# Cross-attention with a routed expert layer on one core: each head's division and transposition moved a slot further back, and six other steps moved with them

## What is computed

```python
def attention(q, k, v):                       # once for the image keys, once for the text keys
    scores = jnp.einsum('bqhd,bkhd->bhqk', q, k) / sqrt(HD)
    return jnp.einsum('bhqk,bkhd->bqhd', softmax(scores), v)
q = rms_norm(linear(layernorm(x), q_w, q_b), norm_q_w)
k, k_img = rms_norm(linear(ctx_txt, ...)), rms_norm(linear(ctx_img, ...))
x = x + linear(attention(q, k, v) + attention(q, k_img, v_img), o_w, o_b)
w = softmax(layernorm(x) @ Wg + bg);  topv, topi = top_k(w, 2)
x = x + sum over the two experts of topv * (W3(gelu(W2(gelu(W1 layernorm(x))))))
```

## Time and profile before

| | us |
|---|---|
| median of 3 runs (837.31 to 839.81) | 837.37 |
| the profiled execution, its own time | 834.9 |
| its span | 832.7 |
| TensorE busy in the span (93%) | 770.6 |
| VectorE busy (72%) | 599.6 |
| ScalarE busy (59%) | 490.9 |
| GpSimd busy (29%) | 240.4 |

### The profile page before, as it was taken

How to read it: one execution, slowest core, us unless ns; L and a number is a source line. 1 busy time by engine, 2 the same in 40 slices (tenths; PEclk the granted TensorE clock), 3 DMA queues, 4 the chain that set the end, 5 groups by cost and what they waited for, 6 DMA issues and landing times.

```text
span 832.7 us, 17460 instructions
## 1 busy us (share of the span) xinstructions
PE 770.6 (93%) x5995; PEld 666.4 (80%) x5995; DVE 599.6 (72%) x1269; ACT 490.9 (59%) x1136; POOL 240.4 (29%) x302
## 2 busy tenths in 40 slices
PE   4889898999999989787899999999999999999994
PEld 3667676767676767555798999999999999999993
DVE  6767878787978787776676757676676758676664
ACT  4377777767676777786245555554545555554543
POOL 3523334342434333223300505032140505032010
PEclk9989999999999999999999999999999999999998
DMA  9820102011020201142756665748566665648561
GB/s 308 291 83 4 56 6 58 38 35 61 24 72 13 83 13 35 31 175 89 260 203 223 233 232 208 248 172 285 191 248 220 238 233 210 250 172 286 194 220 64
DMA packets 29205, 126.28 MB, mean 152 GB/s; under 512 B 4204, under 2 KB 4220, under 8 KB 19424
## 3 DMA queue, kind: packets, MB, share of 16 engines
q1 hardware_dynamic: 23696, 109.80, 37.6%
q0 software_dynamic: 5456, 15.81, 5.3%
HBM read 108.42 MB, written 18.74 MB: 153 GB/s over the span
## 4 chain that ended last, share of the span: by engine, by line
PE 71%; DVE 11%; ACT 10%; issue 4%; DMA 1%; POOL 0%; SPq 0%; ACTq 0%; DVEq 0%; POOLq 0%
PE tiles L1176 6%; PE tiles L1178 6%; PE tiles L1177 6%; PE scores L1478 4%; PE scores L1480 4%; PE scores L1479 4%; PE ptb L1291 4%; PE pvb L1178 3%; PE pvb L1177 3%; PE ptb L1177 3%; PE pvb L1176 3%; PE ptb L1176 3%; PE ptb L1178 3%; PE scores L1281 2%; ACT scr L658 2%
## 5 line engine op out<-in xcount | busy, mean ns | idle before, releaser
L920 DVE TENSOR_TENSOR w<-scr,w 128x2048 fp32r<-128x2048 f32 x75 | 170.8, 2288 | 59.5 <-ACT w L684 59.5
L684 ACT ACTIVATE w<-scr 128x2048 fp32r<-128x2048 f32 x76 | 144.8, 1909 | 54.8 <-PE scores L1480 54.8
L514 POOL DMA_INDIRECT out_dram<-scr,tok x17 | 18.0, 1058 | 298.7 <-DVE scr L1155 296.2
L666 ACT ACTIVATE scr<-scr,rsum 112x257 f32<-112x257 f32 x128 | 66.7, 521 | 60.6 <-DVE rsum L904 60.6
L1176 PE MATMUL tiles<-w 128*128 128x256 f32 (+1 forms) x288 | 82.9, 288 | 0.6
L1176 PE MATMUL tiles<-c,w 128*128 128x258 f32 (+2 forms) x272 | 79.3, 291 | 2.6 <-DVE c L1129 1.2
L1177 PE MATMUL tiles<-w 128*128 128x256 f32 (+1 forms) x288 | 81.2, 282 | 0.0
L1178 PE MATMUL tiles<-w 128*128 128x256 f32 (+1 forms) x288 | 81.2, 282 | 0.0
L1143 DVE CAST w<-scr 128x256 fp32r<-128x256 f32 (+1 forms) x144 | 41.9, 291 | 52.5 <-ACT scr L774 52.5
L1178 PE MATMUL tiles<-c,w 128*128 128x258 f32 (+2 forms) x272 | 76.9, 283 | 0.0
L1177 PE MATMUL tiles<-c,w 128*128 128x258 f32 (+2 forms) x272 | 76.7, 282 | 0.0
(11 more groups left out here) (223 smaller groups left out, 2332.0 us busy)
## 6 DMA issues: line engine op xcount, KB each, us to landing
scr<-in_dram SPq DMA_DIRECT2D x76, 1024.0 KB, 4.9
scr<-in_dram SPq DMA_DIRECT2D x8, 750.0 KB, 4.6
scr<-slots_d SPq DMA_DIRECT2D x10, 528.0 KB, 5.4
scr<-in_dram SPq DMA_DIRECT2D x10, 512.0 KB, 8.8
slots_d<-rows SPq DMA_DIRECT2D x8, 528.0 KB, 11.1
xn<-in_dram SPq DMA_DIRECT2D x9, 256.0 KB
xb<-in_dram SPq DMA_DIRECT2D x8, 224.0 KB, 2.7
xr<-in_dram SPq DMA_DIRECT2D x8, 224.0 KB, 2.6
```

The source lines that it names most:

```text
L666: act.activation(probs[0:L, s, 0:IMG], probs[0:L, s, 0:IMG], ACT.Copy, scale=rsum[0:L, g, s, 0:1]).then_inc(S["normal_img"], 1)
L684: act.activation(EH[slot], raw[slot], ACT.Copy).then_inc(S["eh_done"], 1)
L920: dve.tensor_tensor(EL[slot], raw[slot], EH[slot].bitcast(F32), ALU.subtract).then_inc(S["el_done"], 1)
```

## The change

`LAG` becomes 3. In slot `h` VectorE still inverts head `h-1`, but ScalarE divides head `h-2`, TensorE transposes head `h-3` and ScalarE copies that one out. With it move: the value products of the first two groups from slots 6 and 10 to 7 and 11, of the third from 14 to 15, of the fourth from slot 2 to 3 of the next body; the logits, in bodies 1 to 6, from slot 15 to 14, ahead of the third value product instead of behind it; the rank from ahead of slot 3's projection to behind it; its reading on VectorE from slot 3 to 4, the scatter on GpSimd from slot 4 to 5. No instruction is added or taken away.

```diff
-LAG = 2
+LAG = 3
...
-BUSY_AT = {LAST: {h: 2 for h in range(1, 16)}, DONE: {0: 2, 1: 2, 2: 4, 6: 11, 12: 2, 15: 8}}
-LOGITS_AT = lambda b: 13 if b == LAST else 15
+BUSY_AT = {LAST: {h: 2 for h in range(1, 16)}, DONE: {0: 2, 2: 2, 3: 4, 6: 11, 12: 2, 15: 8}}
+LOGITS_AT = lambda b: 13 if b == LAST else 15 if b == DONE else 14
...
# GpSimd
-                    if h == 3 and has_tail(b):
-                        attended_high(b - 1, 3)
+                    if h in (0, 4) and has_tail(b):
+                        attended_high(b - 1, 2 + h // 4)
...
-                    if h == (8 if fixed(b, DONE) else 4) and has_route(b):
+                    if h == (8 if fixed(b, DONE) else 5) and has_route(b):
...
                         scatter(b - 2)
-                    if h in (7, 11, 15) and has_heads(b):
-                        attended_high(b, (h - 7) // 4)
+                    if h in (8, 12) and has_heads(b):
+                        attended_high(b, (h - 8) // 4)
...
# ScalarE
-                    if h == 0 and has_tail(b):
-                        normalise(b - 1, NH - 1)
-                    if h and has_heads(b):
-                        normalise(b, h - 1)
+                    if h < LAG - 1:
+                        if has_tail(b):
+                            normalise(b - 1, NH - LAG + 1 + h)
+                    elif has_heads(b):
+                        normalise(b, h - LAG + 1)
...
# VectorE
-                    if h in (6, 10, 14) and has_heads(b):
-                        attended(b, (h - 6) // 4)
+                    if h in (0, 4) and has_tail(b):
+                        attended_low(b - 1, 2 + h // 4)
+                    if h in (7, 11) and has_heads(b):
+                        attended(b, (h - 7) // 4)
...
-                    if h in (7, 11, 15) and has_heads(b):
-                        attended_low(b, (h - 7) // 4)
+                    if h in (8, 12) and has_heads(b):
+                        attended_low(b, (h - 8) // 4)
...
-                    if h == 2 and has_tail(b):
+                    if h == 3 and has_tail(b):
                         attended(b - 1, 3)
-                    if h == 3 and has_tail(b):
-                        attended_low(b - 1, 3)
...
+                    if h == 15 and has_heads(b):
+                        attended(b, 2)
...
-                    if h == (7 if fixed(b, DONE) else 3) and has_route(b):
+                    if h == (7 if fixed(b, DONE) else 4) and has_route(b):
                         gate_slots(b - 2)
...
# TensorE
-                if g == (2 if fixed(b, LAST) else 3) and has_tail(b):
+                if g == 2 and has_tail(b):
                     pe.wait_ge(S["lg_done"], b)
...
-                    if h == 2 and has_tail(b):
+                    if h == 3 and has_tail(b):
                         attend(b - 1, 1 - p, 3)
-                    if h in (6, 10, 14) and has_heads(b):
-                        attend(b, p, (h - 6) // 4)
+                    if h in (7, 11) and has_heads(b):
+                        attend(b, p, (h - 7) // 4)
...
                         pe.wait_ge(S["xt_done"], b)
-                        pe.wait_ge(S["a_done"], NC * b + (2 if fixed(b, LAST) else 3) * has_heads(b))
+                        pe.wait_ge(S["a_done"], NC * b + 2 * has_heads(b))
+                        if has_prep(b):
+                            pe.wait_ge(S["rb_read"], b + 2)
...
-                    if h == (6 if fixed(b, DONE) else 3) and has_route(b):
+                    if h == 15 and has_heads(b):
+                        attend(b, p, 2)
+                    if h == 6 and fixed(b, DONE):
                         pe.wait_ge(S["a_done"], NC * b)
                         rank(b - 2)
...
-                    if fixed(b, DONE) and h == 0:
+                    if fixed(b, DONE) and h == 1:
                         stage("o", 0, 3, b, p)
...
+                    if h == 3 and has_route(b) and not fixed(b, DONE):
+                        pe.wait_ge(S["a_done"], NC * b)
+                        rank(b - 2)
```

## The result

The changed kernel takes 852.81 us (median of 6 runs, 851.41 to 859.48), the kernel before 837.86 beside it: ratio 1.0191, 95% interval 1.0165 to 1.0218. It is slower by almost four times what I forecast, and lies outside my range. The profiled execution took 851.4, its span is 849.5, 16.8 more than before.

The account below looks back on a forecast made before the run. TensorE was taken as the bound in bodies 1 to 6, with VectorE deciding where it stops, and ScalarE in body 7. Bodies 1 to 6 +5.6, body 7 -1.7, sum +3.9 us on 837.37: 841.3 us, range 830 to 848.

Parts of the forecast that it names:

- Slots 12 to 15, +1.15: Last quarter of a body: third value product waits 2.1 us, lower clock adds 0.73; +1.15 us a body.
- the rival with the whole block: Slots 12 to 15: GpSimd's cast blocks VectorE for all 1.05 us, +0.43 a body, 843.9 us in all; chance 0.20.
- Slots 0 to 3, -0.9: First quarter of a body: the rank's 0.50 us wait goes, the slot 2 transposition's 0.52 mostly; -0.9 us a body.
- Slots 4 to 7, +0.3: Second quarter: `kx` waits 0.7 us for the rank's bank, `xT` no longer waits 0.32; +0.3 us a body.
- Slots 8 to 11, +0.35: Third quarter: value product no longer covers ScalarE's copy, so the next transposition waits; +0.35 us a body.
- Body 7 and after, -1.7: Last image: ScalarE's 2.21 and 1.57 us waits for inverses shrink, a later last transposition adds 0.93; -1.7 us.
- the slower one, 843.9: Slots 12 to 15: cast blocks VectorE for its whole 1.05 us, +2.6 us in all, 843.9; chance 0.20.

Follow-up runs that it names:

- e7_last_lag2: Changed kernel with the last image alone back at the old lag, its value products in slots 6, 10 and 14: 853.67 us, ratio 1.017.
- a1_after_fill: Changed kernel with more idle matrix products (9, 8, 5 and 4) in the last image's slots 1, 9, 13 and 14: 848.22 us, ratio 1.013.

## Why the prediction was wrong

- **Slots 12 to 15, +1.15**: right in sum (+1.06) by luck, from two errors. The wait stood where I put it, for the reading behind the key scaling, but was 2.62, not 2.1. Of the 0.52, 0.26 is the time from the end of VectorE's reading (172.45 + 0.15) to the product (172.86), which I had at nothing; 0.17 is that TensorE was there earlier than I had it; 0.13 is a longer scaling (171.02 to 172.45, 1.43 in place of 1.30); the reading itself was 0.05 shorter. The cast's block itself costs 0.79: body 6 without the cast, and the run with the cast held back, each have that much less. I had priced it at 0.62, the rival with the whole block at 1.05. The Trainium skill's rule (SBUF — State Buffer, "Who interferes with whom"), which I gave 0.20, has the mechanism right: the cast took 2.03 us behind the splits, then the scaling 1.26 behind the cast. The quarter at the full clock, 13.18, thus met the rival's bound without its price. I had also given body 6 a cast to meet, and it has none. The clock fell in two bodies, not five: 0.28 a body ((14.24 + 13.80 - 2 x 13.18) / 6) in place of 0.73.
- **Slots 0 to 3, -0.9**: the step that failed. I took TensorE's waits for the rank and the transposition as time to be won. The first went, the second stayed, and 0.67 at `kt` came. Bodies 2 to 6 won nothing in the mean (10.89 us against 10.87; bodies 2, 3 and 5, whose clock stayed up, 0.17), and body 1, which has no rank and was to win 0.4, lost 1.25 at `k0`. The runs show why: VectorE has next to no idle time from the queries' scaling in slot 13 to the fourth product's copy in slot 3; with the early reading of the logits, four orders on VectorE and ScalarE gave the same 16.2 us up to that copy. The change took nothing from that queue, the same 47 instructions, and added to it 0.52 and 0.43 of waiting and the longer block. I had written that VectorE decides where TensorE stops, and then counted TensorE's stops all the same. Over bodies 1 to 6 this term, forecast as -0.9 x 5 - 0.4 = -4.9 and measured as +0.22 x 6 = +1.3, is off by 6.2 us.
- **Slots 4 to 7, +0.3**: right (+0.25); `kx` waits 0.46 where I had said 0.7, `qt` 0.39 that I had not.
- **Slots 8 to 11, +0.35**: the wait in slot 11 is the one forecast (0.39); the quarter lost 0.63. The kernels with the old lag and the rank in its old place stay at 9.99 and 10.00, all with the new lag at 10.62 or more, so the lag alone is enough for it; the rank's move alone brings as much with the old lag, by a wait for VectorE. From start to start the stop costs 0.56, not the 0.39 that TensorE is idle: the matmul ahead of the transposition starts 0.79 us before it (157.56 to 158.35), where it was 0.23 (198.92 to 199.15). I had counted only up to the copy's end, 0.33, and a semaphore's delay. 1.7 us in all.
- **Body 7 and after, -1.7**: failed, by 4.2 us. I counted ScalarE's waits for the inverses as its path; they went, but in their place ScalarE waits 3.00, 2.34 and 1.25 us for transpositions, TensorE still waits for ScalarE's copies (1.97, 1.64, 0.91 and 0.58 us), and the clock fell at three of these stops, which I had at nothing. With the waits filled, the step is 63.10 against 62.65: +0.45, still no gain.
- **The rivals**: the slower one, 843.9, had the right mechanism with too high a price (1.05 for 0.79) and went into a sum whose other terms were wrong.

## What to carry to other kernels

Before counting an engine's wait as time to be won, ask whether the engine that ends it has idle time between the last point where it waited itself and there: if it has none, only what leaves its queue counts. Parts of a reordering are not to be priced one by one: here the lag alone costs 4.2%, the logits alone 3.0%, the rank alone nothing, the lag with either of the other two 3.0%, all together 1.9%. Where an engine stands behind stops with nothing to do, idle work that fits into the stops can be worth some us: 5.9, 3.0 and 0.9 behind the last image in the three kernels here.

## What the runs showed of the hardware

- A GpSimd cast that began at 169.97 while VectorE's splits followed one another took 2.03 us in place of 1.05; then VectorE's scaling took 1.26 in place of 0.48. Both engines lose in one meeting.
- A VectorE division with one large input (112 x 118, f32, by a value per row) took 1.08 us beside that cast and 0.28 without. I had only thought of instructions with two inputs; the Trainium skill (SBUF — State Buffer, "Who interferes with whom") counts this kind of instruction among those that can contend, and the trace agrees.
- Bodies 1 to 5 of the changed kernel each have the same stop of 2.62 us. Behind it the clock fell in bodies 3 and 5, in bodies 1 and 4 of the two kernels that differ in the last image only (e7_last_lag2 and a1_after_fill), and in all five with the rank put back. There the rank waits another 1.41 us in bodies 2 to 6; body 1 has no rank. So the stop alone doesn't decide; that the second stop does, and not the longer body, isn't shown.
